# Eight-group decoder step: first head of the next group inside the second attention, and set-up shared between ScalarE and VectorE

## What is computed

```python
qr = q * phase; kr = k * phase            # rotation by t * omega
E = exp(clip(-mu * |t_i - t_j|, -30, 0))  # decay, per head
maha = max(qn + E*E*kn - 2*E*s, 0) / V    # V = sigma/(2 mu) (1 - E*E) + eta + gamma
logits = coef * log1p(maha / nu) - 0.5 * 64 * log(V);  A = softmax(causal(logits))
```

## Time and profile before

| | us |
|---|---|
| three runs | 2319.32, 2320.72, 2329.82; median 2320.72 |
| profiled execution: its time, its span | 2324.63, 2322.8 |
| busy: PE, DVE, ACT, POOL | 1902.5 (82%), 1679.9 (72%), 1111.7 (48%), 844.3 (36%) |
| chain that ended last | DVE 38%, PE 36%, issue 12%, ACT 6%, POOL 6%, DMA 2% |

### The profile page before, as it was taken

How to read it: one execution, slowest core, us unless ns; L and a number is a source line. 1 busy time by engine, 2 the same in 40 slices (tenths; PEclk the granted TensorE clock), 3 DMA queues, 4 the chain that set the end, 5 groups by cost and what they waited for, 6 DMA issues and landing times.

```text
span 2322.8 us, 39833 instructions
## 1 busy us (share of the span) xinstructions
PE 1902.5 (82%) x14136; PEld 1351.3 (58%) x14136; DVE 1679.9 (72%) x4128; ACT 1111.7 (48%) x3149; POOL 844.3 (36%) x766
## 2 busy tenths in 40 slices
PE   1796588978897898888897898878897798777798
PEld 1465356844576456755685467745685467655464
DVE  8895796578947795679847895769757894735355
ACT  3463166435663466435652456435653466334343
POOL 0563274316613363316513462326521662311000
PEclk8997799979997999979997999889997999879799
DMA  3000010401030010402040011202040012324000
GB/s 131 15 1 10 10 64 6 130 11 38 36 110 26 21 62 6 130 10 74 1 123 13 24 60 50 86 16 68 1 130 15 18 56 86 121 78 121 10 14 23
DMA packets 72491, 116.56 MB, mean 50 GB/s; under 512 B 7822, under 2 KB 46870, under 8 KB 71782
## 3 DMA queue, kind: packets, MB, share of 16 engines
q1 hardware_dynamic: 66758, 100.90, 13.6%
q0 software_dynamic: 5536, 13.12, 1.9%
...
## 4 chain that ended last, share of the span: by engine, by line
DVE 38%; PE 36%; issue 12%; ACT 6%; POOL 6%; DMA 2%; SPq 0%; DVEq 0%; POOLq 0%; ACTq 0%
PE bank L1501 33%; DVE work L530 11%; DVE bank L539 5%; DVE work L548 3%; DVE work L528 3%; ACT work L1056 3%; POOL hid L1411 2%; DVE max L841 2%; PE bank L1505 2%; POOL work L1391 1%; ACT act_row L1056 1%; POOL work L1386 1%; DVE acc L750 1%; DMA hid<-y_sorted,slot_id 1%; DVE norm_t_st L460 1%
## 5 line engine op out<-in xcount | busy, mean ns | idle before, releaser
L1501 PEld LDWEIGHTS bank<-work 128*128 128x128 f32 (+2 forms) x5152 | 386.5, 199 | 163.7 <-issue 161.2
L1501 PE MATMUL bank<-work 128*128 128x128 f32 (+2 forms) x5152 | 417.5, 306 | 50.5 <-DMA work<-in_wo 26.2
L1056 ACT ACTIVATE work<-bank 128x512 f32<-128x512 f32 (+1 forms) x560 | 247.0, 519 | 276.0 <-PE bank L1501 243.6
L530 DVE TENSOR_TENSOR work<-bank,table_space 64x512 f32<-64x512 f32 x512 | 352.2, 688 | 6.8
L1379 POOL TENSOR_TENSOR work<-work 128x512 f32<-128x512 f32 x128 | 163.5, 1278 | 328.4 <-DVE work L530 228.0
L1056 ACT ACTIVATE work<-work 128x512 f32<-128x512 f32 (+1 forms) x338 | 196.7, 618 | 139.6 <-DVE work L618 67.6
L1056 ACT ACTIVATE work<-work,negmax 128x128 f32<-128x128 f32 x512 | 199.2, 390 | 100.2 <-DVE negmax L550 100.2
L1386 POOL TENSOR_TENSOR work<-sb_ident,nrm 128x512 f32<-128x512 f32 x128 | 133.3, 1041 | 279.0 <-ACT nrm L1056 279.0
L1501 PE MATMUL bank<-work,table_space 128*128 128x512 f32 x256 | 140.4, 630 | 90.0 <-DVE negmax L550 59.5
L528 DVE TENSOR_TENSOR work<-bank,table_space 128x512 f32<-128x512 f32 x256 | 173.9, 679 | 31.7 <-POOL work L1391 18.2
L1056 ACT ACTIVATE hid<-bank,w_ring 128x128 f32<-128x128 f32 x480 | 136.3, 370 | 123.4 <-PE bank L1501 123.3
...
## 6 DMA issues: line engine op xcount, KB each, us to landing
...
```

The lines of the kernel that those rows point to most:

```text
L530: last = v.tensor_tensor(rows(wk[i + 1][o]), rows(src[p]), sinT[o, s].unsqueeze(1).broadcast_to([DH0, GB, N]), ALU.mult)
L1056: return nc.scalar.activation(o, i, f, **k)
L1501: return nc.tensor.matmul(o, l, r, start=start, stop=stop, skip_group_check=True)
```

## The change

Three edits. **Set-up:** ACT makes the angles, the squares of `dec` and the 16 logarithms per head, and folds the sign into the sine and a quarter turn into the cosine; DVE has one correction step of the angles less. What DVE does for `wgt`, `bias_t`, `q_scale` and four fills becomes `decay_tables`, called between the rotations of heads 0 and 1 of the first group. `fold` uses banks 4 to 7, so PE goes on to the first queries without waiting for ACT; POOL loads x first of all and no longer waits for `cleared` ahead of the slots. **First head:** for groups 0 to 5 slot 0 of the next first attention moves into `attn1`: PE's projections stand between `scores2_T(3)` and `heads2(2)`, DVE's rotation ahead of line 857, POOL's additions and ACT's squares at the end of `attn1`; the tail moves a slot later (slots 1 to 4). `token_ranks` moves up, ahead of `heads2(1)`, and uses bank 2; `ring2` is in another order for it. **Order on PE in all slots:** `norms_of` goes ahead of `keys_of`, `tail_mix` behind the scores.

```diff
-        ring2 = [bank[i] for i in (3, 4, 5, 0, 1, 2)]
+        ring2 = [bank[i] for i in (3, 4, 0, 1, 5, 2)]
...
-            for h in range(H0):
-                last = v.tensor_scalar(ang[:, h], tramp[:], res["freq"][:, h:h + 1], None, ALU.mult)
-            link(last)
             dve.wait_ge(par_a, 3)
-            link(v.tensor_tensor(bias_t[:], dec[:], dec_inv[:], ALU.mult))
-            link(v.tensor_scalar(bias_t[:], bias_t[:], -1.0, 2.0, ALU.mult, ALU.add))
-            link(v.tensor_tensor(dec_inv[:], dec_inv[:], bias_t[:], ALU.mult))
-            link(v.tensor_tensor(bias_t[:], dec[:], dec[:], ALU.mult))
-            for h in range(H0):
-                last = v.tensor_scalar(bias_t[:, h], bias_t[:, h], neg_amp[:, h:h + 1], base[:, h:h + 1],
-                                       ALU.mult, ALU.add)
-            last.then_inc(par_v, 1)
             link(v.tensor_scalar(turns, ang, 1 / (2 * math.pi), MAGIC, ALU.mult, ALU.add))
             link(v.tensor_scalar(turns, turns, -MAGIC, None, ALU.add))
             link(v.scalar_tensor_tensor(red, turns, -C1, ang, ALU.mult, ALU.add))
             link(v.scalar_tensor_tensor(red, turns, -C2, red, ALU.mult, ALU.add))
-            link(v.scalar_tensor_tensor(red, turns, -C3, red, ALU.mult, ALU.add))
-            link(v.tensor_scalar(red, red, PI, -PI, ALU.min, ALU.max))
-            v.tensor_scalar(turns, red, math.pi / 2, -2 * math.pi, ALU.is_gt, ALU.mult).then_inc(par_v, 1)
-            dve.wait_ge(par_v, 4)
-            link(v.scalar_tensor_tensor(turns, red, math.pi / 2, turns, ALU.add, ALU.add))
-            v.tensor_scalar(turns, turns, PI, -PI, ALU.min, ALU.max).then_inc(par_v, 1)
+            v.tensor_scalar(red, red, PI, -PI, ALU.min, ALU.max).then_inc(par_v, 1)
+            dve.wait_ge(par_v, 3)
+            v.scalar_tensor_tensor(turns, red, -1.0, red, ALU.mult, ALU.min).then_inc(par_v, 1)
+            dve.wait_ge(par_a, 4)
+            link(v.tensor_tensor(wgt[:], dec[:], dec_inv[:], ALU.mult))
+            link(v.tensor_scalar(wgt[:], wgt[:], -1.0, 2.0, ALU.mult, ALU.add))
+            v.tensor_tensor(dec_inv[:], dec_inv[:], wgt[:], ALU.mult).then_inc(par_v, 1)
             link(v.reciprocal(rnu, nu))
             link(v.tensor_scalar(rnu, rnu, -2.0, None, ALU.mult))
-            v.memset(v1[:], 1.0)
-            v.memset(m_parts[:], 0.0)
-            v.memset(m2_parts[1][:], 0.0)
-            v.memset(tok[:], 0.0)
-            dve.wait_ge(par_a, 4)
-            for h in range(H0):
-                last = v.scalar_tensor_tensor(wgt[:, h], dec[:, h], rnu[:, h:h + 1], wgt[:, h], ALU.mult, ALU.mult)
-            link(last)
-            mask_b = mask_ij[:].unsqueeze(1).broadcast_to([128, H0, N])
-            link(v.scalar_tensor_tensor(bias_t[:], bias_t[:], -0.5 * DH0, mask_b, ALU.mult, ALU.add))
             dve.wait_ge(loaded, 16 * len(rest))
-            v.tensor_copy(sel24[:], res["sel24"])
+            link(v.tensor_copy(sel24[:], res["sel24"]))
             v.tensor_tensor(res["gate_w"][:, 1], res["gate_w"][:, 1], res["gate_w"][:, 2], ALU.add)
-            dve.wait_ge(par_a, 6)
-            v.tensor_scalar(sinT[:], sinT[:], sgn, None, ALU.mult).then_inc(tables, 1)
-            dve.wait_ge(tables, 1)
+            dve.wait_ge(fold, 4)
+            dve.wait_ge(par_a, 7)
+            def decay_tables():
+                sc = DH2 ** -0.5
+                link(v.tensor_scalar(q_scale[:], p_sig[:, H0:H0 + 1], -sc, None, ALU.mult))
+                link(v.tensor_tensor(q_scale[:], q_scale[:], top_rows, ALU.mult))
+                link(v.scalar_tensor_tensor(q_scale[:], low_rows, sc, q_scale[:], ALU.mult, ALU.add))
...
+                v.memset(tok[:], 0.0).then_inc(tables, 1)
+                dve.wait_ge(par_a, 8)
+                for h in range(H0):
+                    last = v.scalar_tensor_tensor(wgt[:, h], dec[:, h], rnu[:, h:h + 1], wgt[:, h], ALU.mult, ALU.mult)
+                link(last)
+                mask_b = mask_ij[:].unsqueeze(1).broadcast_to([128, H0, N])
+                link(v.scalar_tensor_tensor(bias_t[:], bias_t[:], -0.5 * DH0, mask_b, ALU.mult, ALU.add))
...
+                v.tensor_copy(slot[:], rank_in).then_inc(rank_read, 1)
+                dve.wait_ge(rank_read, tally(g, d, 1, 1))
...
+                begun = 1 if heads and tail else 0
                 between = {}
                 if tail:
-                    between = {0: lambda: tail_out(g, d - 2), 2: lambda: centre_of(norm_t, g, 2, d - 2)}
-                for s in range(H0 + 5):
+                    between = {begun: lambda: tail_out(g, d - 2), begun + 2: lambda: centre_of(norm_t, g, 2, d - 2)}
+                for s in range(begun, H0 + 5):
...
+                    if g == 0 and not experts and s == 0:
+                        decay_tables()
+                    if tail and s == begun:
                         centre_of(norm_t, g, 1, d - 2)
-                    if tail and s == 1:
+                    if tail and s == begun + 1:
                         tail_mix(g, d - 2)
-                    if tail and s == 3:
+                    if tail and s == begun + 3:
                         tail_logits(g, d - 2)
...
+                if first_head:
+                    attn0_slot(0, g, 2)
...
+            for h in range(H0):
+                last = fn(ang[:, h], tramp[:], ACT.Copy, scale=res["freq"][:, h:h + 1])
+            last.then_inc(par_a, 1)
             act.wait_ge(par_v, 2)
-            link(fn(dec_inv[:], dec[:], ACT.Exp, scale=-1.0))
-            fn(dec[:], dec[:], ACT.Exp).then_inc(par_a, 1)
+            fn(dec_inv[:], dec[:], ACT.Exp, scale=-1.0)
+            link(fn(dec[:], dec[:], ACT.Exp))
+            fn(bias_t[:], dec[:], ACT.Square).then_inc(par_a, 1)
+            act.wait_ge(par_a, 4)
+            for h in range(H0):
+                last = fn(bias_t[:, h], bias_t[:, h], ACT.Ln, scale=neg_amp[:, h:h + 1], bias=base[:, h:h + 1])
+            last.then_inc(par_a, 1)
             act.wait_ge(par_v, 3)
-            link(fn(bias_t[:], bias_t[:], ACT.Ln))
+            fn(sinT[:], red, ACT.Sin, scale=sgn).then_inc(par_a, 1)
+            act.wait_ge(par_v, 4)
+            fn(cosT[:], turns, ACT.Sin, bias=cols[:, 7:8]).then_inc(par_a, 1)
+            act.preload_act_table_set("natural_log_exp_and_others")
+            act.wait_ge(par_v, 5)
+            act.wait_ge(par_a, 5)
             fn(wgt[:], bias_t[:], ACT.Exp, scale=-1.0).then_inc(par_a, 1)
-            act.wait_ge(par_v, 4)
-            fn(sinT[:], red, ACT.Sin).then_inc(par_a, 1)
-            act.wait_ge(par_v, 5)
-            fn(cosT[:], turns, ACT.Sin).then_inc(par_a, 1)
-            act.preload_act_table_set("natural_log_exp_and_others")
             for c in range(4):
                 act.wait_ge(fold, c + 1)
-                fn(vo[:, 4 * c:4 * c + 4].rearrange("p h d -> p (h d)"), bank[c][:], ACT.Copy).then_inc(fold_sb, 1)
+                fn(vo[:, 4 * c:4 * c + 4].rearrange("p h d -> p (h d)"), bank[4 + c][:], ACT.Copy).then_inc(fold_sb, 1)
...
+                if begun:
+                    act.wait_ge(o2, g * SLOTS)
+                    square(0, g, d)
                 for s in range(DRAIN):
-                    if tail and s == 1:
-                        norm_tail(g, 1, bank[2], act_row[1], d - 2)
+                    if begun and s == 1:
+                        norm(norm_t, g, 1, ahead=d - 2)
+                    if tail and s == begun + 1:
+                        norm_tail(g, 1, bank[2], act_row[1], d - 2, begun)
                         t_to_T(g, 1, bank[7], d - 2)
-                    if tail and s == 2:
+                    if tail and s == begun + 2:
                         norm_tail(g, 2, bank[6], act_row[0], d - 2)
                     if heads:
-                        attn0_slot(s, g, d)
-                    if tail and s == 2:
+                        attn0_slot(s, g, d, begun and s == 1)
...
+            def first_head(g):
+                pool.wait_ge(o2, g * SLOTS + 3)
+                attn0_slot(0, g, 2)
...
+            load_x(0)
             pool.wait_ge(loaded_first, 16 * len(for_tables))
             pool.wait_ge(loaded, 16 * len(rest))
-            load_x(0)
+            heads(0, 0, False, False)
             pool.wait_ge(cleared, 16 * LOAD)
-            heads(0, 0, False, False)
...
-                    last = mm(rows(bank[c])[:, h % 4], res["wvT0"][:, h], res["wo0"][:, h], start=h % 4 == 0)
+                    last = mm(rows(bank[4 + c])[:, h % 4], res["wvT0"][:, h], res["wo0"][:, h], start=h % 4 == 0)
                 last.then_inc(fold, 1)
-            pe.wait_ge(fold_sb, 4)
...
-                    if heads and s < H0:
+                    if heads and begun <= s < H0:
                         queries_of(s, g, d)
+                    if g == 0 and not experts and s == 2:
+                        pe.wait_ge(fold_sb, 4)
+                    if heads and 0 <= s - 2 < H0:
+                        norms_of(s - 2, g, d)
+                    if heads and begun <= s < H0:
```

(26 more changed lines are left out.)

74 lines of the change are left out of this document (39 added, 35 removed).

## The result

The changed kernel takes 2285.65 us in the median of four runs (2280.35 to 2291.94), the kernel before 2322.97 beside it (2319.32 to 2329.82): ratio 0.983, 95% interval 0.9804 to 0.9857. I had said 2278, 2262 to 2300, and faster. The profiled execution is the slowest of the four, 2291.94 with a span of 2290.1, so its parts are worth some 6 us less than the median. Lines have moved: 519, 528, 539, 683 and 857 of before are 505, 514, 525, 669 and 849 now.

What follows compares the result with a forecast made beforehand. The chain alternates between VectorE and TensorE. Gains 18.5 + 21 + 2.8 + 0.4 = 42.7 off the profiled 2324.63 give 2281.9; the median lies 3.9 below that execution, so 2278 us, range 2262 to 2300.

Steps and rivals of the forecast that it cites:

- Set-up: Start up to the first completion of scores: gain 18.5 us, ends 16 to 19.5.
- first rotation: Set-up, head 0 on VectorE: starts at 33.8 us in place of 54.84, right after `fold` and the first queries.
- head 2's queries: Set-up on TensorE: run at 1.2 GHz after idling most of 8 us, taking 2.08 us; 1.0 us of loss booked.
- first completion: VectorE's first completion of scores (line 539) comes at 56.0 us in place of 74.53.
- ScalarE's per-head instructions: Set-up: 16 angles and 16 logarithms of 128 x 128, angles at 0.375 us each, 6.0 us per 16.
- `decay_tables`: VectorE between the rotations of heads 0 and 1: 8.7 us, work moved rather than hidden, `q_scale` about 0.2 net.
- GpSimd's wait for the stores: Set-up: no longer waiting for the stores of zeros (`cleared`), which held head 1 back, gives 3.5 of the 18.5 us.
- First head: Groups 0 to 5, `attn1` and the slots behind: 4.17 - 1.6 + 1.0 = 3.5 us gained per group, 21 in all.
- the waits in the tail's slots: VectorE in slots behind `attn1`: 3.0 us of waits in place of 4.0, so 1.0 gained per group.
- the new order on TensorE: `norms_of` before `keys_of`: gains nothing in the steady slots of the first attention, which stay at 7.59 us.
- Low clock: Line 857 to the steady part: one of two low TensorE clock stretches goes, 2.8 us gained, ends 5.5 and -5.5.
- 0.4 of gain: Group 6, with only the earlier `token_ranks`: line 857 starts 0.4 us earlier.

Runs made afterwards that it cites:

- old_order: Changed kernel with TensorE's transposes of the norms behind the key projection again, as before: 2302.59 us, ratio 0.991 to the kernel before.
- order_alone: Kernel before with one edit, `norms_of` ahead of `keys_of` on TensorE: 2328.78 us, ratio 1.004 to the kernel before.
- fill_experts: Changed kernel with spare, unread TensorE products in the pauses of two down projections: 2281.10 us, ratio 0.982 to the kernel before.
- wt_tables_fill: Changed kernel with a later wait for the router weights' copy, decay tables before the first rotation, spare products in two down projections: 2271.13 us, ratio 0.978.
- The kernel with both kinds of spare products: Changed kernel with later router-weights wait, decay tables first, spare TensorE products in two down projections and around the second attention: 2261.85 us, ratio 0.974.

## Why the prediction was right, and which terms were mis-sized

**Set-up.** 18.5 predicted, 19.4 measured, and the steps held: first rotation 33.8 predicted, 32.21 (`fold` 25.21 + 6.10); head 2's queries at 1.2 GHz as booked (2.07); first completion 56.0 predicted, 55.56. ScalarE's per-head instructions took 0.30 and 0.39 where I had 0.375. `decay_tables` was 9.7 and not 8.7: I had `q_scale` at about 0.2 net, and one of its instructions took 1.14. GpSimd's wait for the stores was worth 2.8 of the 3.5. Head 2's queries did run at 1.2 GHz, but the clock had fallen before the idle stretch of 8.26 to which I had put it down. It is 1.00 from 30 to 36 and 0.50 from 36.9 to 40, head 1's keys took 1.75 at 36.48, and TensorE had waited only 1.33 and 1.00 until then. The rule in the Trainium skill, "TensorE: Matmul & The Clock Gate", "What's actually happening" (throttled unless active), agrees with the low clock at 48.34; it didn't tell me of the earlier fall.

**First head.** Line 849 comes 15.57 after the router choice at full clock where line 857 came after 13.89: 1.7 lost, 1.6 predicted. From there 31.26, 32.0 predicted. Per group 4.1 against 3.5. The size was near, the account was not: I booked the waits in the tail's slots at 4.0 to 3.0 and said of the new order on TensorE that it gains nothing in the steady slots. That is so (7.59 everywhere), but in the tail's slots it decides: 2.7 of the 4.1, by old_order. And it only does so together with the first head (0.5 alone), so the split of the 4.1 depends on which edit comes first. I had not followed GpSimd's diagonal back to the transposes.

**Low clock.** This is the step that failed: "PE has now fewer pauses in this stretch, so I count one of the two low stretches as gone: 2.8", with ends of -5.5 and 5.5. The two stretches inside boundaries did go. But the clock is low in other places: in five of six boundaries the low stretch of the second attention now reaches over the router choice (some 1.5 us each; it did so in one of before), and three expert parts and the last stage had new ones. From the parts: 19.4 + 0.9 + 6 x 4.13 = 45.1 was earned and 32.7 arrived, so the clock cost 12.4 in the profiled execution; in the medians 45.1 - 37.3 = 7.8. (The 0.9 holds a low stretch too: five kernels with the new order take 202.6 to 202.8 there, not 204.49.) The forecast's sum was 39.9 without the clock, 5.2 too small, and the clock 2.8 up in place of 8 to 12 down; the two errors partly cancelled, so that the total came out 8 from the forecast is in part luck. The clock's loss is missing in the range as well: 16 + 12 + 0.4 of gain, less 5.5, gives 2298, and the 2292 that I wrote is the sum without the 5.5. What I had not seen is that the new order, booked at nothing in the steady slots, stands in every group part and brings falls of the clock there (old_order 9.0 less in these parts, order_alone 12.9 more).

**Shown and not shown.** That the falls in expert parts need the pauses of 0.48 and 1.11 is shown as far as one profiled execution of each kernel can: filled, they are gone in all 21 groups of the three kernels with `fill` there. That a fall costs some 3 us is read from the group parts (207.4 against 204.5, 2.9) and from TensorE's rows (from 914.80 to 926.29 in group 2, from 661.93 to 670.30 in group 1 for the same work, 3.1). The pauses alone don't bring a fall: the kernels with the old order have them (0.48 or 0.49, and 1.11) in all 21 groups and no fall. Why the same pauses lower the clock in one group and not in the next is open; the program and the pauses are the same. The Trainium skill, "TensorE: Matmul & The Clock Gate", "What's actually happening", says that the chip's activity monitor runs free and is not reset when a kernel starts, which would let the same pause count in one group and not in the next; no run here tests it. fill_experts gained less in its median than three falls would give, and wt_tables_fill nothing, so other low stretches move when these go. The kernel with both kinds of spare products is a gain that I can't divide between fewer falls and a faster second attention beyond the 1 us per group above.
